# Graph layer on one core: the second lot's sort keys kept in halves in PSUM and SBUF

## The reference

```python
xn = layernorm(x)
h = xn @ W                                   # 6250 x 64
el, er = h @ Wl.T, h @ Wr.T                  # 4 heads
e = exp(leaky_relu(el[src] + er[dst], 0.2))  # one row for each edge
w = e / segment_sum(e, src)[src]
gnn = elu(stack([segment_sum(w[:, k:k+1] * h[dst], src) for k in range(4)]) + b)
mix = rmsnorm(linear_attention(rmsnorm(xn)) @ w_out + b_out) + xn
x = x + gnn + mix
out = x + mixture_of_8_experts_top2(layernorm(x))
```

## Time and profile before

| | |
|---|---|
| three runs | 3689.47, 3703.99, 3711.27 us, median 3703.99 |
| profiled execution | 3743.12 us, its span 3741.3 us |
| TensorE matmuls, weight loads busy | 1924.2 us (51%), 1603.5 us (43%) |
| VectorE busy | 2055.8 us (55%) |
| ScalarE busy | 1934.9 us (52%) |
| GpSimd busy | 1837.5 us (49%) |
| gathers, line 1667 | 1612, 1634.3 us busy, 1455.4 us of idle time before them |
| mean granted clock of TensorE | 0.575 |

### The profile page before, as it was taken

The page is one execution under the profiler, slowest core; times in us unless marked ns, Lnnn a source line. Parts: engine busy times, 40 slices in busy tenths (PEclk is TensorE's granted clock), DMA queues, the critical chain, the costliest instruction groups (busy, mean ns, idle before and its releaser), DMA issues.

```text
span 3741.3 us, 48709 instructions
## 1 busy us (share of the span) xinstructions
PE 1924.2 (51%) x8560; PEld 1603.5 (43%) x8561; DVE 2055.8 (55%) x4630; ACT 1934.9 (52%) x6577; POOL 1837.5 (49%) x1826
## 2 busy tenths in 40 slices
PE   3732361055555556555545455445455448358884
PEld 1322231055544555444434444444444447347663
DVE  8981788355555555445445444444444448674344
ACT  2542141166666666556546555555555558464431
POOL 0047588734344434543446666666666660054434
PEclk8965675555555555555555555555555555559997
DMA  8011112212222222222211111111111110424554
GB/s 263 10 36 39 40 34 57 52 49 48 56 47 55 57 55 49 55 60 56 53 29 24 24 24 24 23 24 24 23 25 24 23 23 3 119 95 145 157 156 147
DMA packets 162143, 215.76 MB, mean 58 GB/s; under 512 B 47363, under 2 KB 117307, under 8 KB 161794
## 3 DMA queue, kind: packets, MB, share of 16 engines
q0 software_dynamic: 60992, 82.75, 11.9%
q1 hardware_dynamic: 93712, 124.09, 10.9%
q10 hardware_dynamic: 7346, 7.92, 0.7%
HBM read 128.60 MB, written 79.49 MB: 56 GB/s over the span
## 4 chain that ended last, share of the span: by engine, by line
issue 29%; DVE 23%; another core or an unknown queue 20%; PE 16%; ACT 6%; DVEq 4%; ACTq 1%; DMA 1%; SPq 0%; POOL 0%; POOLq 0%
PE ps L1236 5%; DVE ps L866 5%; DVE arena L701 4%; DVE big L890 4%; DVE arena L702 3%; PE ps L1312 3%; PE ps L1328 2%; DVEq L511 1%; ACT arena L1498 1%; PE ps L1195 1%; DVEq L890 1%; ACT arena L1487 1%; DVEq L888 1%; PE ps L1320 1%
## 5 line engine op out<-in xcount | busy, mean ns | idle before, releaser
L1667 POOL DMA_INDIRECT arena<-gather_table,arena x1612 | 1634.3, 1014 | 1455.4 <-DMA staged_rows<-arena 525.4
L1236 PE MATMUL ps<-arena 128*128 x4784 | 1124.9, 420 | 814.2 <-DVE big L890 394.3
L1236 PEld LDWEIGHTS ps<-arena 128*128 128x128 f32 x4784 | 1055.8, 329 | 894.1 <-issue 893.1
L1498 ACT ACTIVATE arena<-lane,arena 128x32 f32<-128x32 f32 x2392 | 566.2, 313 | 475.8 <-issue 258.0
L890 DVE TENSOR_TENSOR big<-ps,big 128x65 f32 x1196 | 262.1, 219 | 930.5 <-remote 650.7
L866 DVE TENSOR_TENSOR ps<-ps,arena 128x512 f32<-128x512 f32 x598 | 387.9, 695 | 284.4 <-remote 141.0
L1476 ACT ACTIVATE arena<-ps 128x1024 f32<-128x1024 f32 x299 | 304.4, 1018 | 261.3 <-DVE ps L874 165.5
L1226 PE MATMUL ps<-el,pick_w 48*128 x1196 | 205.2, 294 | 394.6 <-issue 361.6
L874 DVE TENSOR_TENSOR ps<-ps,arena 128x1024 f32<-128x1024 f32 x299 | 366.2, 1225 | 21.4 <-remote 21.4
L879 DVE TENSOR_TENSOR arena<-ps,arena 128x1024 f32<-128x1024 f32 x299 | 363.5, 1216 | 4.6 <-issue 3.3
L1487 ACT ACTIVATE arena<-arena 128x2 f32 x1196 | 258.7, 286 | 143.7 <-issue 117.5
(11 more groups left out here) (292 smaller groups left out, 1914.8 us busy)
## 6 DMA issues: line engine op xcount, KB each, us to landing
staged_rows<-arena SPq DMA_DIRECT2D x48, 552.0 KB
arena<-staged_rows SPq DMA_DIRECT2D x48, 552.0 KB
arena<-gather_table,arena POOLq DMA_INDIRECT x1612
arena<-slot_rows SPq DMA_DIRECT2D x119, 128.0 KB
expert_rows<-arena SPq DMA_DIRECT2D x119, 128.0 KB
slot_rows<-ends_w SPq DMA_DIRECT2D x2, 4480.0 KB, 25.5
arena<-big SPq DMA_DIRECT2D x112, 56.9 KB
slot_rows<-ends_w SPq DMA_DIRECT2D x1, 6272.0 KB, 33.0
```

The lines of the kernel that those rows point to most:

```text
L1236: ins = pe.matmul(ps[:, 6 + u % 2, i * AW:i * AW + AW], share_w[u % 4][:, (i * GT + c) * P:(i * GT + c + 1) * P], gat[:, bass.ds(place["ag ...
L1498: ins = act.activation(away[par][:, j, :], lane[:, 0:WN], ACT.Square, bias=loc[par][:, j:j + 1], scale=FAR)
L1667: pool.indirect_dma_start(rows, None, table_d, bass.IndirectOffsetOnAxis(ap=dst_x[:, t:t + 1], axis=0)).then_inc(s_gat[p % LAND], 16)
```

## The change

The first lot gets five blocks and 17 levels, the second eight blocks and 17 levels. From its first enter on, the second lot is sorted by a new function, `both_step`. It keeps the keys in two halves of 512 columns, by the bit that the next plain step compares: elements with this bit 0 in a bank of PSUM (`low_keys`), the others in SBUF, so that a plain step has one input in PSUM and one in SBUF. Its results go out already divided by the bit after that: four instructions of 256 elements a step, after a wait for the whole step before. The last plain step before an enter writes all keys to SBUF, in two halves of four blocks. The banks of the transposes are exchanged for it. The pairs that go by DRAM are 448 instead of 384 (56 chunks), the first fetches come after spill 13 instead of 11 and the fifth after spill 17 instead of 15, then four fetches to five spills instead of 31 to 40. POOL waits for all spills not at the first direct pair but 13 pairs later (`CLEAR`).

```diff
--- before.py
+++ after.py
@@ -147,7 +147,7 @@
     REST = E - FULL - ROWS * P
 
 
-    LOTS = ((0, 4, 16, ((0, 4),)), (4, NB - 4, 18, ((0, 4), (4, NB - 4))))
+    LOTS = ((0, 5, 17, ((0, 5),)), (5, NB - 5, 17, ((0, 4), (4, NB - 5))))
     CUT = LOTS[0][1] * BLK
 
 
@@ -175,10 +175,13 @@
     PC = -(-NP // P)
     STAGE, STAGES = 8, 3
     RINGA = RING // 2
-    NPS = 384
+    NPS = 448
     NST = NPS // STAGE
 
-    FETCH_AT = [11 + n if n < 4 else 15 + (n - 3) * 31 // 40 for n in range(NST)]
+    CLEAR = T * HID // (GT * (HD + C + 1)) - RINGA
+    assert CLEAR > 0
+
+    FETCH_AT = [13 + n if n < 4 else 17 + (n - 3) * 4 // 5 for n in range(NST)]
     assert E == (NP - 1) * GT * P + E % (GT * P) and NB * BLK >= NP * GT * P + GI * GT * P and P * IC >= NG * GI and P * PC >= NP
     RW = HD * AW
     WST = TS * QW
@@ -474,7 +477,11 @@
             return v[:, LOTS[lot][0]:LOTS[lot][0] + LOTS[lot][1], :]
 
 
-        turned = [ps[:, a:b, :].rearrange("p a (b m) -> p (a b) m", m=P)[:, 0:LOTS[lot][1], :] for lot, (a, b) in enumerate(((0, 1), (1, 4)))]
+
+        turned = [ps[:, b:b + 2, :].rearrange("p a (b m) -> p (a b) m", m=P)[:, 0:LOTS[lot][1], :] for lot, b in enumerate((2, 0))]
+        HALF = LOTS[1][1] * P // 2
+        assert 2 * HALF == 1 << LOTS[1][2] - ROW_BITS and HALF == 512
+        low_keys = [ps[:, 2 + c, :] for c in range(2)]
 
         def part_of(j):
             return max(p for p in range(len(PARTS)) if SLOT0[p] <= j)
@@ -728,6 +735,77 @@
                 keys_done[lot], parts_done[lot] = m, done
                 at[lot, kind, side, k, j] = (list(done), keys_in[lot])
 
+            def place_bit(n_):
+
+                _, side, _, j = plans[1][n_]
+                return j if side == "A" else j - ROW_BITS
+
+            def both_step(n_):
+
+
+
+                _, nb, levels, halves = LOTS[1]
+                kind, side, k, j = plans[1][n_]
+                key, m, done, cur = s_key[1], keys_done[1], list(parts_done[1]), keys_in[1]
+                q, l = place_bit(n_), 1 << place_bit(n_)
+                kept = n_ + 1 < len(plans[1]) and plans[1][n_ + 1][0] == "plain"
+                full = [blocks(keys[c], 1).rearrange("p t m -> p (t m)") for c in range(2)]
+                low, high = low_keys[cur], full[cur][:, 0:HALF]
+                to_low, to_high, to_full = low_keys[1 - cur], full[1 - cur][:, 0:HALF], full[1 - cur]
+                assert not kept or place_bit(n_ + 1) == q - 1
+
+                if kind == "plain":
+                    dve.wait_ge(key, m)
+                    if kept:
+                        for v, to in enumerate((to_low, to_high)):
+                            al, ah = [x.rearrange("p (g v l) -> p g v l", v=2, l=l // 2)[:, :, v, :] for x in (low, high)]
+                            o = to.rearrange("p (g b l) -> p g b l", b=2, l=l // 2)
+                            dve.tensor_tensor(o[:, :, 0, :], al, ah, ALU.min).then_inc(key, 1)
+                            dve.tensor_tensor(o[:, :, 1, :], al, ah, ALU.max).then_inc(key, 1)
+                            m += 2
+                        done = [m] * len(halves)
+                    else:
+                        for h, (t0, t1) in enumerate(halves):
+                            al, ah = [x[:, t0 * P // 2:t1 * P // 2].rearrange("p (g l) -> p g l", l=l) for x in (low, high)]
+                            o = to_full[:, t0 * P:t1 * P].rearrange("p (g b l) -> p g b l", b=2, l=l)
+                            dve.tensor_tensor(o[:, :, 0, :], al, ah, ALU.min).then_inc(key, 1)
+                            dve.tensor_tensor(o[:, :, 1, :], al, ah, ALU.max).then_inc(key, 1)
+                            m += 2
+                            done[h] = m
+                else:
+                    parts = ((0, nb),) if side == "B" and k > 2 * ROW_BITS else halves
+                    for h, (t0, t1) in enumerate(parts):
+                        entered[1] += 1
+                        dve.wait_ge(s_right[1], entered[1])
+                        left = turned[1].rearrange("p t m -> p (t m)")[:, t0 * P:t1 * P]
+                        rite = blocks(right, 1).rearrange("p t m -> p (t m)")[:, t0 * P:t1 * P]
+
+                        runs = (0,) if side == "A" else (1,) if k == levels else (-1, 1)
+                        nd = len(runs)
+                        for d, sign in enumerate(runs):
+                            for v in range(2 if kept else 1):
+                                if kept:
+                                    al = left.rearrange("p (g d b v l) -> p g d b v l", d=nd, b=2, v=2, l=l // 2)[:, :, d, 0, v, :]
+                                    ah = rite.rearrange("p (g d b v l) -> p g d b v l", d=nd, b=2, v=2, l=l // 2)[:, :, d, 1, v, :]
+                                    o = (to_low, to_high)[v][:, t0 * P // 2:t1 * P // 2].rearrange("p (g d b l) -> p g d b l", d=nd, b=2, l=l // 2)[:, :, d, :, :]
+                                else:
+                                    al = left.rearrange("p (g d b l) -> p g d b l", d=nd, b=2, l=l)[:, :, d, 0, :]
+                                    ah = rite.rearrange("p (g d b l) -> p g d b l", d=nd, b=2, l=l)[:, :, d, 1, :]
+                                    o = to_full[:, t0 * P:t1 * P].rearrange("p (g d b l) -> p g d b l", d=nd, b=2, l=l)[:, :, d, :, :]
+                                for b_, op in enumerate((ALU.min, ALU.max)):
+                                    if sign == 0:
+                                        dve.tensor_tensor(o[:, :, b_, :], al, ah, op).then_inc(key, 1)
+                                    else:
+                                        x0, x1 = (al, ah) if sign > 0 else (ah, al)
+                                        dve.scalar_tensor_tensor(out=o[:, :, b_, :], in0=x0, scalar=-1.0, in1=x1, op0=ALU.mult, op1=op).then_inc(key, 1)
+                                    m += 1
+                        done[h] = m
+                    if len(parts) == 1:
+                        done = [m] * len(halves)
+                keys_in[1] = 1 - cur
+                keys_done[1], parts_done[1] = m, done
+                at[1, kind, side, k, j] = (list(done), keys_in[1])
+
             def sorted_lot(lot):
 
                 b0, nb = LOTS[lot][0:2]
@@ -753,12 +831,13 @@
                             sort_step(1, ahead)
                             ahead += 1
                 sort_step(0, n_)
+            assert ahead == alone
             at["sorted", 0] = keys_done[0], keys_in[0]
             sorted_lot(0)
             turns_ = 0
             for n_ in range(ahead, len(plans[1])):
                 kind, side, k, j = plans[1][n_]
-                sort_step(1, n_)
+                both_step(n_)
                 turns_ += kind == "enter"
                 if kind == "enter" and 0 <= turns_ - 2 - ROWS_AT < len(CHUNKS):
                     add_rows(turns_ - 2 - ROWS_AT)
@@ -1648,7 +1727,7 @@
                     pool.wait_ge(s_agg, 1)
                 if p == NPA:
                     pool.wait_ge(s_step, at["dst", 1])
-                if p == NPS:
+                if p == NPS + CLEAR:
                     for r in s_spill:
                         pool.wait_ge(r, 16 * (NST // 2))
                 if p >= LAND:
```

## The result

Beside the kernel before, whose median was 3705.51 us (4 runs, 3689.47 to 3711.27), the changed kernel took 3837.84 us (4 runs, 3832.11 to 3843.88): ratio 1.0346, 95% interval [1.0322, 1.0369]. The forecast was 3657 us and faster; the time lies outside its range, on the other side.

What follows compares the result with a forecast made beforehand. Bound: the groups' own 5.0 us plus a toll on each gather in the loop. Sort -6, then -18 - 24 + 12 - 11, sum -47 us: 3743.12 to 3696 profiled, times 0.9895 gives 3657 us; range 3610 to 3790.

Steps and rivals of the forecast that it cites:

- Lot 0 +34: First lot's sort: five blocks and 17 levels for four and 16 add 34 us, on the path.
- The block up to the stop +30: Second lot's sort until the gathers stop at 409 us: moves as a block, +34 less one locked gather, +30 us.
- The last level -30.7: Second lot's sort: its last level goes, saving 30.7 us.
- the steps and enters -5: Second lot's remaining sort: plain steps of 1.46 us for 1.48 and cheaper enters together save 5 us.
- The gathers ahead: Before the first group: one gather every 1.25 us, 318 done for 269 before, up to 336 allowed.
- rival A: The toll moves into the second lot's sort: 206 unlocked gathers at 0.74 us each; 3789 us, 3865 at 1.11; chance 0.21.
- -18: Loop's slow start: 18 gathers left for 35, at 1.06 us each, saves 18 us.
- -24: Loop: 32 gathers leave it at 0.74 us each, saving 24 us (21 to 36).
- +12: 448 pairs by DRAM: 128 gathers move from a toll of 0.65 to 0.74 us, costing 12 us.
- -11: Later spill wait: 26 gathers move into GpSimd's idle time, at 0.7 for 1.11 us, saving 11 us (0 to 25).
- Rival B: Second lot's sort: the lock on gathers stays, 138 gathers before the first group; slower, 3729 us; chance 0.07.
- Rival C: Gathers taken out of the loop were covered by data waits; no difference, 3699 us; chance 0.17 with other small outcomes.

Runs made afterwards that it cites:

- in B: Condition of five measurements, cause open: kernel before takes 2924 to 2931 us, changed kernel 0.9701 of it; other engines' instructions do not come late beside unbroken gathers.
- In A: Condition of three measurements, the first included, cause open: kernel before takes 3705 to 3747 us; other engines' instructions come late while gathers run unbroken.
- halves_only: Changed kernel with lots of five and eight blocks and halves in PSUM, but 384 pairs, old fetches, old spill wait: 3875.67 us for 3739.51, 1.0358.
- lots_only: Kernel before with only the cut into five and eight blocks (and exchanged transpose banks), whole keys, sort_step: 3750.74 us for 3746.81, 1.0017.

## Why the prediction was wrong, step by step

**Lot 0 +34**: right, 249.2 for 214.9, +34.3.

**The block up to the stop +30**: the gathers resumed at 447.98 for 409.37, +38.6. Nearly.

**The last level -30.7, the steps and enters -5**: as lengths of the code these were right. Plain steps are 1.46 us apart, as forecast, and in B, where nothing else acts on them, the sort ends at 563.3 for 564.7, -1.4, where the sum had said -6. In A the stretch from the resumed gathers to the end of the sort took 405.3 us (447.98 to 853.3), where 235.7 (409.37 to 645.1) less 35.7 gives 200, and where the same instructions took 202.5 in B.

**The gathers ahead**: one every 1.25 us, as forecast, and 336 ahead of the loop for a forecast of 318.

**The step that failed** is the one between these two: that 206 gathers, freed from the lock, come beside the sort for nothing. It was named, as rival A, and given 0.21. The 224 gathers after 447.98 cost 405.3 - 200 = 205 us, 0.92 us each; the rival's bounds were 0.74 and 1.11, its times 3789 and 3865 us, and the time measured is 3838. What I held against it was a row of 41 small VectorE instructions 0.2 us apart amid gathers. That row was taken soon after locked gathers (one of 3.71 us at 673.00), and the changed kernel shows 25 us of full pace after a pause: it was no evidence about a long unbroken run. The rows from 296 to 378 us, where gathers had run unbroken for long, were, and the sort's steps should have been priced by them. A toll that is paid in the loop at 0.65 to 0.74 us was treated as one of the loop. In A it comes with unbroken gathers in the sort as well, and in before the lock had thinned them there: 157 gathers in 293.7 us.

**The loop**: forecast -18 - 24 + 12 - 11 = -41, measured -101.9 (-44.1 in halves_only against lots_only, -63.6 from there to the changed kernel). 61 gathers more are done before the first line 953 (336, and 275 before the first line 874): at 0.73 us, the mean of before's loop, they explain 45 us. The unbroken run with two groups in 80 us is gone: in 1800 to 1900 us there are 13 groups and 48 gathers. The later wait was sized at -11 with -25 as its end. Some 57 us are left for it and the 448 pairs together, of which up to 31.6 may be the long profiled execution of before. The parts weren't told apart in A, so how far the terms -24, +12 and -11 were off stays open.

**Rival B**, the lock stays: no. Gathers beside `both_step` in PSUM took 0.94. One of 6.55 us, at 464.61, ran beside line 648 of the attention, a single VectorE instruction of 6.69 us with both inputs in SBUF. **Rival C**, no difference: no.

**The range** ended at 3790 since it took in rival A at its lower toll only. With 0.21 on A the upper toll belonged in it.

That the time under B is 0.970 does not make the forecast right: it was of the 3703.99 us, by rows of that condition, and even in B the reasons are others. Nothing of the -91 us there comes from fewer gathers in the loop; it is the chain of gathers, in which only the lock (-91.4), the later start (+33.1) and the standing still (-32.9) count. The 10.07 us gather had been seen, but its price was worked out as gathers per stretch, not as time on the path, as it isn't there in A.

## What to carry to other kernels

A stall can be a shield. Before an engine is freed from a lock, ask what its freed instructions do to those who ran undisturbed while it was held, and price that by the stretch in which it ran unbroken for longest, not by the mean. A price per instruction that was read in one phase holds for the condition it was read in; look for a stretch of the trace in which the suspected cause is off and the same code runs. And measure the kernel before anew in each measurement: here it moved by a fifth with no instruction changed, and the order of the same two kernels turned with it. Before a gap is put down to "issue", count whether the trace still holds the events that would name another cause.

## What was not expected of the hardware

- The same program at 3741.3 and 2922.3 us of span.
- In A, a plain step of four VectorE instructions every 4.90 us for 1.46 us, beside gathers every 1.25 us; set in after 25 us of them.
- The same program leaves 20,063 semaphore events in the trace in A and 45,637 in B, and equally many, 1273, up to the end of lot 0's sort, before the first gather.
- One indirect gather of 36.07 us beside a run of min and max in SBUF without waits, and 10.28 us beside steps in interleaved halves, but at most 2.60 us beside steps of four with a full wait.
- The wait for the spills before the first direct gather, taken for a price of its place, hangs on both edits: 47.54 us in A and 27.5 in B for the kernel before, 5.4 in B with 448 pairs and the wait where it was.
